# Routing weights ahead of batch 0, block sums between weight splits, and a copy that waits for three matmuls instead of nine

## What is computed

```
masked_w = weight * mask[None, :, :]
w_bot = einsum('bg,got->bot', y, masked_w)
x = x + einsum('bnt,bot->bno', x, w_bot) + bias

rw = softmax(cond_8); w, sel = top_k(rw, 2); w = w / w.sum(-1)
w = scale * w + (1 - scale) * w            # scale = 1/12
mlp(x) = (gelu(x @ gate) * (x @ up)) @ down
x = x + sum over the 2 selected experts of w * mlp_e(x) + mlp_shared(x)
```

## Time and profile before

| | |
|---|---|
| median of 3 runs | 418.2 us (418.14 to 418.57) |
| the profiled execution: its own time | 416.81 us |
| its span (first to last instruction) | 415.0 us |
| TensorE busy | 408.6 us, 98% of the span |
| VectorE busy | 296.0 us, 71% |
| ScalarE busy | 249.8 us, 60% |
| GpSimd busy | 296.4 us, 71% |
| granted clock of TensorE | 1.00 |
| DMA, mean | 85 GB/s |
| chain that ended last | PE 88%, POOL 4%, DVE 4%, DMA 1%, issue 1% |

### The profile page before, as it was taken

How to read it: one execution, slowest core, us unless ns; L and a number is a source line. 1 busy time by engine, 2 the same in 40 slices (tenths; PEclk the granted TensorE clock), 3 DMA queues, 4 the chain that set the end, 5 groups by cost and what they waited for, 6 DMA issues and landing times.

```text
span 415.0 us, 7355 instructions
## 1 busy us (share of the span) xinstructions
PE 408.6 (98%) x2241; PEld 354.5 (85%) x2241; DVE 296.0 (71%) x511; ACT 249.8 (60%) x484; POOL 296.4 (71%) x322
## 2 busy tenths in 40 slices
PE   8999999999999999999999999999999999999997
PEld 6778788888888888888888888888888888888886
DVE  3589997666667877766767878776676675666684
ACT  6576586665655567665556566666465555766541
POOL 1599899998608859989733877998661885878630
PEclk9999999999999999999999999999999999999999
DMA  7742432333200442224210053322300033232101
GB/s 249 237 141 83 126 103 80 100 101 81 74 27 0 127 127 78 77 80 129 56 42 1 24 178 84 97 97 76 101 25 25 2 100 104 76 94 86 42 10 54
DMA packets 19615, 35.23 MB, mean 85 GB/s; under 512 B 2178, under 2 KB 2946, under 8 KB 19586
## 3 DMA queue, kind: packets, MB, share of 16 engines
q1 hardware_dynamic: 19296, 34.61, 27.9%
q10 hardware_dynamic: 290, 0.26, 0.2%
HBM read 32.77 MB, written 2.10 MB: 84 GB/s over the span
## 4 chain that ended last, share of the span: by engine, by line
PE 88%; POOL 4%; DVE 4%; DMA 1%; issue 1%; SPq 1%; ACT 1%; DVEq 0%; POOLq 0%
PE o_ps L548 15%; PE p_ps L548 11%; PE g_ps L494 10%; PE g_ps L493 10%; PE g_ps L497 10%; PE u_ps L493 10%; PE u_ps L497 10%; PE u_ps L494 10%; PE l_ps L449 2%; DMA l_raw<-l_w 1%; POOL sg_lo L1154 1%; DVE l_ps L954 1%; POOL sd_lo L1185 1%; DVE h_lo L1018 1%; PE p_ps L430 1%
## 5 line engine op out<-in xcount | busy, mean ns | idle before, releaser
L1158 POOL TENSOR_TENSOR eg_lo<-raw_g,eg_hi 128x512 fp32r<-128x512 f32 x64 | 92.5, 1466 | 12.6 <-ACT eg_hi L689 12.6
L982 DVE SCALAR_TENSOR_TENSOR u_ps<-gelu,route_cur,u_ps 128x512 f32<-128x512 f32 x64 | 48.3, 754 | 54.3 <-PE u_ps L497 52.1
L718 ACT ACTIVATE gelu<-g_ps 128x512 f32<-128x512 f32 x95 | 57.2, 602 | 36.8 <-PE g_ps L497 36.3
L1018 DVE TENSOR_TENSOR h_lo<-t_raw,h_hi 128x1024 fp32r<-128x1024 f32 x46 | 67.8, 1475 | 1.1 <-ACT h_hi L746 1.1
L740 ACT CAST h_hi<-u_ps 128x512 fp32r<-128x512 f32 x46 | 27.0, 587 | 69.2 <-DVE u_ps L982 41.2
L1198 POOL TENSOR_TENSOR ed_lo<-raw_d,ed_hi 128x384 fp32r<-128x384 f32 x30 | 31.8, 1061 | 31.0 <-ACT ed_hi L698 31.0
L494 PE MATMUL g_ps<-x_hi,eg_lo 128*128 128x512 f32 (+1 forms) x128 | 50.6, 395 | 0.0
L493 PE MATMUL u_ps<-x_hi,eg_hi 128*128 128x512 f32 (+1 forms) x128 | 49.9, 390 | 0.4 <-DVE h_lo L1008 0.4
L493 PE MATMUL g_ps<-x_hi,eg_hi 128*128 128x512 f32 (+1 forms) x128 | 50.2, 392 | 0.0
L494 PE MATMUL u_ps<-x_hi,eg_lo 128*128 128x512 f32 (+1 forms) x128 | 49.8, 389 | 0.0
L746 ACT CAST h_hi<-t_raw 128x1024 fp32r<-128x1024 f32 x46 | 48.2, 1048 | 1.0 <-DVE t_raw L1004 0.9
(11 more groups left out here) (226 smaller groups left out, 1153.7 us busy)
## 6 DMA issues: line engine op xcount, KB each, us to landing
raw_g<-experts SPq DMA_DIRECT2D x64, 256.0 KB, 2.8
raw_d<-experts SPq DMA_DIRECT2D x32, 256.0 KB, 2.7
l_raw<-l_w SPq DMA_DIRECT2D x8, 256.0 KB, 5.2
x_in<-xT SPq DMA_DIRECT2D x8, 256.0 KB, 4.3
raw_g<-shared SPq DMA_DIRECT2D x8, 256.0 KB, 4.7
outT<-out_sb SPq DMA_DIRECT2D x6, 256.0 KB, 3.8
raw_d<-shared SPq DMA_DIRECT2D x4, 256.0 KB, 3.3
mask<-l_mask SPq DMA_DIRECT2D x2, 128.5 KB, 5.9
```

Source lines behind the costliest of these rows:

```text
L718: act.activation(gelu[:, s % 2], l0_ps if at_first(b) and s == 1 else g_ps, ACT.Gelu_apprx_tanh).then_inc(gelu_done, 1)
L982: dve.scalar_tensor_tensor(u_ps[:, s % 2], gelu[:, s % 2], route_cur[:, k:k + 1], u_ps[:, s % 2], ALU.mult, ALU.mult).then_inc(h_done, 1)
L1018: dve.tensor_tensor(h_lo[:, at], t_raw[:], h_hi[:, at].bitcast(F32), ALU.subtract).then_inc(t_lo_done, 1)
L1158: pool.tensor_tensor(eg_lo[:, j % RING], raw_g[:, j % RAW_G], eg_hi[:, j % RING].bitcast(F32), ALU.subtract).then_inc(gu_lo_done, 1)
```

## The change

Three edits.

1. VectorE: the eight operations of route_weigh leave steps 3 to 6. The first four (`route_sums`) stand between the split of the masked mix and first_x1_lo, the last four (`route_weigh`) between route_index and the first form_h.
2. GpSimd: shared_s(0) goes from behind split_up(2) to behind split_gate(1), and split_shared_d(0) ahead of split_shared(3). ScalarE: split_shared_s(0) goes from behind activate(0, 1) to behind activate(0, 0).
3. ScalarE's split_b11 waits for a new semaphore, b11_read, which TensorE raises behind the third matmul of P1, instead of for products_123 as a whole; split_b2 gets a wait for products_123 of the pair before, which it had through split_b11.

```
-                product(P1, wt, None, A11, B11, first, last)
+                product(P1, wt, None, A11, B11, first, last).then_inc(b11_read, 1)
                 product(P2, wt, None, A12, B21, first, False)
                 product(P3, wt, None, S4, B22, False, last).then_inc(down_done, 1)
...
                 if not first_pair(b, p):
-                    act.wait_ge(down_done, n - 1)
+                    act.wait_ge(b11_read, pair_count(b, p))
                     act.wait_ge(t_done, 4 * pair_count(b, p))
...
                 act.wait_ge(h_done, n + 1)
+                if not first_pair(b, p):
+                    act.wait_ge(down_done, n - 2)
                 act.copy(h_hi[:, B21 * TH:(B22 + 1) * TH], u_ps[:, 1]).then_inc(h_hi_done, 1)
...
             activate(0, 0)
+            split_shared_s(0)
             split_b11(0, 0)
             weights_beside(0, 0)
             activate(0, 1)
-            split_shared_s(0)
             split_b2(0, 0)
...
-            def route_weigh(s):
-                if s == 3:
...
+            def route_sums():
+                dve.wait_ge(exp_done, 1)
+                dve.reduce_sum(exp_sum[:], exps[:], AX_X).then_inc(weighed, 1)
...
+            def route_weigh():
+                dve.wait_ge(weighed, 4)
+                dve.reciprocal(pair_rsum[:], pair_sum[:]).then_inc(weighed, 1)
...
             def beside(b, s, with_next):
-                if at_first(b):
-                    route_weigh(s)
                 if with_next:
...
             for oh in range(HH):
                 split_l0_0(oh)
+            route_sums()
             for oh in range(HH):
                 first_x1_lo(oh)
             route_index()
+            route_weigh()
...
             def batch_0():
-                for c in range(FIRST):
-                    split_gate(c)
-                    split_up(c)
+                split_gate(0)
+                split_up(0)
+                split_gate(1)
                 shared_s(0)
+                split_up(1)
+                split_gate(2)
+                split_up(2)
+                split_shared_d(0)
                 split_shared(FIRST)
-                split_shared_d(0)
                 for s in range(1, STEPS):
```

More of the change, by code:

```diff
@@ L186, in build @@
         t_lo_done = sem("t_lo_done")
+        b11_read = sem("b11_read")
         down_done = sem("down_done")
@@ new lines, in route_sums @@
+            def route_sums():
+                dve.wait_ge(exp_done, 1)
+                dve.reduce_sum(exp_sum[:], exps[:], AX_X).then_inc(weighed, 1)
+                dve.wait_ge(weighed, 1)
+                dve.reciprocal(exp_rsum[:], exp_sum[:]).then_inc(weighed, 1)
+                dve.wait_ge(weighed, 2)
+                dve.tensor_tensor(probs[:], exps[:], exp_rsum[:].unsqueeze(2).to_broadcast([P, B, 8]), ALU.mult).then_inc(weighed, 1)
+                dve.wait_ge(weighed, 3)
+                dve.tensor_tensor(pair_sum[:], probs[:, :, 0], probs[:, :, 1], ALU.add).then_inc(weighed, 1)
@@ new lines, in route_weigh @@
+            def route_weigh():
+                dve.wait_ge(weighed, 4)
+                dve.reciprocal(pair_rsum[:], pair_sum[:]).then_inc(weighed, 1)
+                dve.wait_ge(weighed, 5)
+                dve.tensor_tensor(pair[:], probs[:, :, 0:TOP_K], pair_rsum[:].unsqueeze(2).to_broadcast([P, B, TOP_K]), ALU.mult).then_inc(weighed, 1)
+                dve.wait_ge(weighed, 6)
+                dve.tensor_scalar(pair_rest[:], pair[:], 1.0 - SCALE, None, ALU.mult).then_inc(weighed, 1)
+                dve.wait_ge(weighed, 7)
+                dve.scalar_tensor_tensor(route_w[:].rearrange("p (b k) -> p b k", k=TOP_K), pair[:], SCALE, pair_rest[:],
+                                         ALU.mult, ALU.add).then_inc(weighed, 1)
```

## The result

| | before | changed |
|---|---|---|
| median beside each other | 418.38 us (4 runs) | 414.53 us (4 runs, 414.20 to 415.76) |
| ratio | | 0.9914, interval 0.9892 to 0.9935 |
| the profiled execution: its own time | 416.81 us | 414.58 us |
| its span | 415.0 us | 412.8 us |
| TensorE busy | 408.6 us | 407.0 us |

The two profiled executions differ by 2.2 us alone. So there are two questions: did the steps that the prediction named go as forecast, and where is the rest.

What follows compares the result with a forecast made beforehand. TensorE was taken as the bound, fully busy from 57 to 400 us, with 2.26 us lost earlier. Terms 0.32 + 1.9 - 0.4 = 1.8 us, from the 418.2 us median, gave 416.4 us, range 415.5 to 417.8.

Steps and rivals of the forecast that it cites:

- Nothing can be gained behind 57 us: TensorE, 57 to 400 us: busy all 343.00 us, no matmul removed, so gains must lie earlier and losses there need new waits.
- 2.26 us are lost between chunks 3 and 10: Batch 0's first steps: 30.44 us against 28.18 undisturbed; VectorE's some 1.9 us and GpSimd's 0.32 us would all go.
- The giveback of 0.4 us: Routing operations ahead of form_h(0,0) wait for two GpSimd splits; TensorE's first product comes 0.4 us later.
- Case A: Rival: routing ahead of form_h(0,0) waits for three splits; first product 1.15 us late, gain 1.1, 417.1 us; chance 0.2.
- B: Rival: the giveback before the first product is hidden, L713 keeping its time; 2.2 us gained, 416.0 us; chance 0.05.
- The sum by the steps: Whole kernel: 0.32 + 1.9 - 0.4 = 1.8 us less.
- TensorE waited for nothing in that stretch, so I cost it at 0: ScalarE's copy of B11: its waits shorten by about 0.7 us each, but the time gains 0.
- holds none of the moved work: The tail after 400 us: set aside as containing no moved work, with no term in the sum.
- It lies 1.4 us below the median of 418.2 us: Profiled execution of the kernel before, 416.81 us: the forecast subtracts its gain from the median instead.
- Case C: Rival: another wait takes the freed time in batch 0's steps; 0.3 to 0.7 us gained, 0.4 lost, 418.0 us; chance 0.1.
- D: Rival: P1's signal costs TensorE 0.08 us in each of 46 pairs of steps; 1.9 us slower, 420.1 us; chance 0.05.
- the rule of the Trainium skill cited in the prediction: VectorE's single-source SBUF operations in two-port mode and GpSimd's exclude each other for whole instructions, so the reciprocal would wait.

Runs made afterwards that it cites:

- e1: Kernel before with only the eight routing operations moved ahead of batch 0's steps on VectorE; 417.15 us, ratio 0.9969.
- e2: Kernel before with only the new orders of GpSimd and ScalarE for the sums of shared block 0; 418.44 us, ratio 1.0000.
- e6: Changed kernel without the new orders of GpSimd and ScalarE, keeping the routing move and the b11_read wait; 415.12 us, ratio 0.9939.
- e9: Changed kernel with route_sums behind combine_0(1), where GpSimd is idle, and route_weigh where route_sums stood; 414.59 us, ratio 0.9919.
- e3: Kernel before with only the b11_read change, the copy of B11 waiting for P1 alone; 416.81 us, ratio 0.9973.
- e5: Changed kernel without the b11_read change, keeping the routing move and the GpSimd and ScalarE orders; 416.44 us, ratio 0.9957.
- e4: Changed kernel run and traced once more, without an edit; 414.67 us, ratio 0.9924 against the kernel before.
- e0: Kernel before run and traced once more, without an edit; 417.61 us, ratio 0.9987 against the same kernel beside it.
- e13: Kernel before with the b11_read wait in batches 0 to 2 only, the last batch as before; 417.05 us, ratio 0.9979.
- e12: Kernel before with the b11_read wait in the last batch only, down_done in the batches before; 416.91 us, ratio 0.9972.
- e7: Kernel before with the b11_read signal raised on P1's third matmul and nobody waiting for it; 418.21 us, ratio 0.9999.
- e11: Changed kernel with e9's routing placement and both writes of x1 ahead of the copy of chunk 4; 413.98 us, ratio 0.9902.

## Why the prediction was wrong

**The direction was right, and so was the mechanism up to chunk 10; the term that failed lies behind the last matmul.** Step by step:

- *Nothing can be gained behind 57 us while TensorE is busy for 343 of 343 us*: right for the matmuls; the stretch from chunk 10 to the last matmul is the same within 0.2 us in all traces.
- *2.26 us are lost between chunks 3 and 10, 1.9 of them for VectorE, 0.32 for GpSimd, and all go*: right in the sum, 0 lost in the changed kernel. The shares are a little off: the step behind the wait for GpSimd is 0.12 us long as well (4.30 in place of 4.18), so GpSimd had 0.44 us and VectorE 1.82. e1 shows that the routing operations alone do it for VectorE, e2 and e6 that the GpSimd part needs both edits.
- *The giveback of 0.4 us*: measured 0.33, by the waits named. Case A did not come about, nor B in the changed kernel; e9 shows B's state (11.88 us) when the last four operations stand elsewhere. The sum by the steps was 1.8 us and the traces have 1.93.
- *b11_read: "TensorE waited for nothing in that stretch, so I cost it at 0"*: **this term failed.** It is right about TensorE's waits (e3 loses 2.25 us up to chunk 10, as before) and wrong about the time: measured 1.1 us by the ratio of e3 (0.27% of 418.2; 1.4 between the medians), 1.77 us between e5 and e4. It is the tail, which the prediction left out in half a sentence ("holds none of the moved work").
- *"It lies 1.4 us below the median of 418.2 us, which is what I predict from"*: **the same fault from the other side.** I saw that the profiled execution was 1.4 us quicker than the median and carried the difference over as if it stayed. It was the thing to explain: that trace had the short tail of 3.2 us, and tails of 4.8 to 4.9 us turn up in five of the seven later traces in which the last batch's copy is late. Neither of the two traces of the kernel before has one, so that its slower runs do is inferred: 73 of 95 runs of it beside e0 to e13 are above 417.6 us, and none of the 23 of e3 and e12. Long less short is 1.6 us. With it the account nearly closes: 1.93 + 1.6 = 3.5 us, against 3.62 between the medians beside e4 and 3.85 at first. It is rough, since the median of the kernel before stands over runs with and without the long tail.
- Case C (another wait in place) and D (the signal costs TensorE) are out: no new wait, and e7 has the signal for nothing.

What is shown is that with edit 3 taken away the long tail comes back (e5 against e4), that the earlier copy in the last batch is enough to be rid of it (e12), and that in all five long tails the last 18 store packets wait for the end of the fetch. No run moved the fetch by itself. Why an earlier copy on ScalarE moves a fetch is open, and so is why the fetch comes so early, 6.4 us ahead of the last matmul, in both traces of the kernel before.

## What to carry to other kernels

Before predicting from a profiled execution, ask why it differs from the median of the timed runs; where the difference is as large as the expected gain, it is a term of the sum, and a second trace of the same kernel costs less than an error of its size. Operations of four columns are not cheap when they depend on one another and each has to wait for a whole instruction of another engine, as here for GpSimd's. In e11 most of them stand where that engine is idle, and the first product comes 0.8 us earlier than where they were merely moved off the bound stretch (with the writes of x1 moved too). And an edit that frees no engine can still move what lies at the very end.

## What the runs showed of the hardware

- One 16 KB packet of the instruction queue among the last stores came with a tail of 4.8 to 4.9 us in place of 3.2 to 3.4: in each of the five such traces 18 of the 576 store packets began only at its end, in e1 from 413.49 us on, the last four of them past 414.4.
- When that packet comes is not set by the programs of VectorE, GpSimd and SyncE alone: with these the same it came 6.4 us ahead of the last matmul (before, e0), or 1.6 us behind it (e7, where TensorE's program has the signal more). Two traces of one kernel agreed closely: both 6.4 us ahead for the kernel before, 0.25 and 0.74 us ahead for the changed one.
- VectorE and GpSimd took turns by whole instructions where VectorE's operation had two tensors in SBUF or was the tensor_scalar: pair_rest and route_w, on 8 columns, took 0.62 and 0.65 us beside GpSimd's splits of 0.74 us, and 0.17 us where it was idle (route_w in e11's order, at 15.32 us). The one-source reciprocal took 0.16 us beside a running GpSimd operation there, and 0.18 us in the earlier trace rows, unblocked; the rule of the Trainium skill cited in the prediction would, as the prediction reads it, have it wait, and for the reciprocal that reading does not hold.
- The first matmul on the masked weights varied from 12.15 to 13.88 us over sixteen traces, up to 1.7 us. It is earlier in the eight traces with edit 1 (12.15 to 12.88, mean 12.60) than in the eight without (12.66 to 13.88, mean 13.18). No edit stands ahead of it but that of e9 and e11, nothing was run to find out why, and the medians do not ask for it: e1 and e5 gain 1.1 and 1.85 us against the runs beside them, and their traces give 0.8 and 1.9 without it.
